# A convolution's norm steps, routed transposes and logits stand elsewhere in the order of a transformer kernel

## What is computed

```python
def conv_mixer(v, k, bias, x1, x2, num_heads):       # v = layernorm(x), x1 = x2 = ctx
    vr, x1r, x2r = (t.reshape(B, H, num_heads, L) for t in (v, x1, x2))
    kv = vr[:, :, :, None, :] * x2r[:, :, None, :, :]
    y = irfft(rfft(kv, n=2 * L) * rfft(k, n=2 * L)[None, :, None, None, :])[..., :L]
    y = y + kv * bias.reshape(H, num_heads)[None, :, :, None, None]
    return jnp.einsum('bhijl,bhil->bhjl', y, x1r).reshape(B, D, L)

x = x + conv_mixer(layernorm(x), L0_xattn_k, fside_S2_0, ctx_2048, ctx_2048, 8)
xn = layernorm(x)
logits = xn @ L0_ffn_gate_w                          # the router: the best 2 of 8 experts per row
x = x + shared_expert(xn) + routed_experts(xn, top2(logits))
x = x + latent_attention(layernorm(x), ctx_2048, itok)
x = x + ffn(layernorm(x))
```

## Time and profile before

| | before |
|---|---|
| time, median of 3 runs (lowest to highest) | 3274.34 us (3273.34 to 3274.57) |
| the profiled execution | 3277.38 us |
| its span, first to last instruction | 3275.6 us |
| PE busy | 3175.7 us (97%) |
| DVE busy | 2173.6 us (66%) |
| ACT busy | 1267.7 us (39%) |
| POOL busy | 1051.4 us (32%) |

### The profile page before, as it was taken

The page is one execution under the profiler, slowest core; times in us unless marked ns, Lnnn a source line. Parts: engine busy times, 40 slices in busy tenths (PEclk is TensorE's granted clock), DMA queues, the critical chain, the costliest instruction groups (busy, mean ns, idle before and its releaser), DMA issues.

```text
span 3275.6 us, 51687 instructions
## 1 busy us (share of the span) xinstructions
PE 3175.7 (97%) x18581; PEld 2699.7 (82%) x18581; DVE 2173.6 (66%) x5817; ACT 1267.7 (39%) x3058; POOL 1051.4 (32%) x1111
## 2 busy tenths in 40 slices
PE   7999999999999889999999999999998999999999
PEld 4666666689899769999999999999997788888887
DVE  6888888756555577778878787777776533333332
ACT  2333333333344345555555555555554311111111
POOL 7877777535211122222222222222201011010110
PEclk9999999999999899999999999999999999999999
DMA  4544443259644521111111111111101300000000
GB/s 129 155 142 133 132 140 95 81 171 313 194 155 151 207 90 53 46 46 46 46 46 40 39 46 46 46 39 40 46 14 44 108 26 26 26 26 26 26 14 13
DMA packets 123780, 267.41 MB, mean 82 GB/s; under 512 B 17689, under 2 KB 18337, under 8 KB 123530
## 3 DMA queue, kind: packets, MB, share of 16 engines
q1 hardware_dynamic: 100122, 186.59, 18.2%
q0 software_dynamic: 23408, 77.51, 7.0%
HBM read 159.49 MB, written 104.56 MB: 81 GB/s over the span
## 4 chain that ended last, share of the span: by engine, by line
PE 79%; DVE 9%; POOL 7%; ACT 1%; DMA 1%; issue 1%; SPq 0%; POOLq 0%; DVEq 0%
PE g_PH L1046 11%; PE g_O L1069 11%; PE t_U L1511 10%; PE t_S L1463 9%; PE t_PO L1498 5%; PE t_M L1447 5%; POOL c_kf L358 3%; PE t_T L1485 3%; PE f_Y L920 3%; PE f_Y L691 3%; PE t_M L1402 2%; PE f_Y L385 2%; PE f_Y L390 2%; DVE c_R L403 2%; DVE c_z L397 2%; PE t_M L1384 2%
## 5 line engine op out<-in xcount | busy, mean ns | idle before, releaser
L1473 ACT ACTIVATE t_pr<-t_sm,t_nb 128x256 f32<-128x256 f32 x512 | 256.5, 502 | 368.5 <-DVE t_nb L1469 368.5
L1059 DVE CAST g_hh<-g_hf 128x512 fp32r<-128x512 f32 x128 | 61.8, 483 | 434.7 <-PE g_O L1069 429.9
L1417 POOL TENSOR_TENSOR t_r<-t_r 128x256 f32<-128x256 f32 x128 | 95.9, 750 | 778.9 <-DVE t_rw L1479 451.7
L358 POOL TENSOR_TENSOR c_kf<-c_vt,c_ct 128x512 f32<-128x512 f32 x256 | 296.6, 1179 | 0.0
L1058 ACT ACTIVATE g_hf<-g_PH,g_b1s 128x512 f32<-128x512 f32 x128 | 88.2, 689 | 519.1 <-PE g_PH L1046 519.1
L1480 DVE TENSOR_SCALAR t_pr<-t_pr,t_rw 128x256 f32<-128x256 f32 x512 | 222.0, 434 | 18.2
L390 PE MATMUL f_Y<-c_kh,c_th 128*128 128x512 f32 x448 | 199.9, 446 | 9.6 <-ACT c_kh L365 9.6
L1046 PE MATMUL g_PH<-g_xh,g_w1h 128*128 128x512 f32 x512 | 205.3, 401 | 1.5 <-DVE g_xl L1034 1.5
L1046 PE MATMUL g_PH<-g_xh,g_w1l 128*128 128x512 f32 x512 | 203.0, 396 | 0.0
L1046 PE MATMUL g_PH<-g_xl,g_w1h 128*128 128x512 f32 x512 | 202.6, 396 | 0.0
L1069 PE MATMUL g_O<-g_w2h,g_hh 128*128 128x512 f32 x512 | 202.3, 395 | 0.0
(11 more groups left out here) (356 smaller groups left out, 9696.1 us busy)
## 6 DMA issues: line engine op xcount, KB each, us to landing
xs<-c_zero SPq DMA_DIRECT2D x71, 256.0 KB, 5.2
f_xg<-xs SPq DMA_DIRECT2D x71, 256.0 KB, 2.8
ys<-f_yt POOLq DMA_DIRECT2D x71, 256.0 KB, 2.4
c_tr<-kpad SPq DMA_DIRECT2D x60, 256.0 KB, 4.8
f_xg<-xn SPq DMA_DIRECT2D x40, 256.0 KB, 4.6
c_xt<-x SPq DMA_DIRECT2D x32, 256.0 KB, 3.5
c_cr<-ctx SPq DMA_DIRECT2D x32, 256.0 KB, 3.9
c_ct<-ctxh SPq DMA_DIRECT2D x32, 256.0 KB, 4.4
```

The source lines that it names most:

```text
L358: T["kv", h] = T["kv1", n] = p.do("gpsimd", lambda e: e.tensor_tensor(o, iv, ic, ALU.mult), g("vt", h), g("ct", h), g("kl", n - 8), g("kh" ...
L1473: T["ex", x] = p.do("scalar", lambda e, t=t, k4=k4: e.activation(pr[:, N % 2, t, :], sm[:, k4, :], ACT.Exp, bias=nb[:, k4, 0:1], scale=-1. ...
```

## The change

`layernorm_stats` is taken apart for the two norms of the convolution: the DVE part (`layernorm_variance`, its first line is 118 in the changed kernel) stays in `stats` and `stats0`, and POOL's power gets functions of its own, `power` and `power0`, that are called a step or more later. `shift(h + 1)` moves from the last step of the head before to the first of this one, `weigh` a step later, `stats` a step earlier; `shift0` and `norm0` stand together behind step 2 of the second half; `turn0` stands ahead of step 3 instead of behind it; `logit` behind step 0 of the first half instead of step 1.

```diff
+def layernorm_variance(p, x, st, ag, rs, tok, free):
+
+    a = p.do("vector", lambda e: e.bn_stats(st, x), tok, free)
+    a = p.do("vector", lambda e: e.bn_aggr(ag, st), a)
+    return p.do("vector", lambda e: e.tensor_scalar(rs, ag[:, 1:2], EPS, None, ALU.add), a)
...
+    def power0(i):
+        s = i % 2
+        U["rs", i] = p.do("gpsimd", lambda e: e.tensor_tensor(rs0[:, s, :], rs0[:, s, :], mhalf, ALU.pow), U["va", i], c_mh)
...
-                if u == 1 and lb == 2 and h + 2 < n_heads:
+                if u == 1 and lb == 1 and h + 2 < n_heads:
                     stats(h + 2)
+                if u == 1 and lb == 3 and h + 2 < n_heads:
+                    power(h + 2)
...
                 if u == 0 and lb == 0 and more:
+                    if h:
+                        shift(h + 1)
                     norm(h + 1)
-                if u == 0 and lb == 0 and more:
+                if u == 0 and lb == 1 and more:
                     weigh(h + 1)
-                if u == 1 and lb == 3 and h + 2 < n_heads:
-                    shift(h + 2)
...
+                if u == 1 and lb == 3 and h:
+                    turn0(h - 1)
                 conv(h, u, lb, units[n] if n < len(units) and lb == 0 else None)
...
+                if u == 0 and lb == 0 and h > 1:
+                    logit(h - 2)
                 if u == 0 and lb == 1:
                     shared_weights()
-                    if h > 1:
-                        logit(h - 2)
...
                 if h and u == 1:
-                    (stats0, shift0, norm0, turn0)[lb](h - 1)
+                    if lb < 3:
+                        (stats0, power0, shift0)[lb](h - 1)
+                    if lb == 2:
+                        norm0(h - 1)
```

More of the change, by code:

```diff
@@ L296, in stats, with power @@
         s = h % 2
-        T["rs", h] = layernorm_stats(p, xt[:, h % 4, :], st[:, s, :], ag[:, s, :], rs[:, s, :], mhalf, g("x", h), g("xn", h - 2), c_mh)
+        T["va", h] = layernorm_variance(p, xt[:, h % 4, :], st[:, s, :], ag[:, s, :], rs[:, s, :], g("x", h), g("xn", h - 2))
+    def power(h):
+        s = h % 2
+        T["rs", h] = p.do("gpsimd", lambda e: e.tensor_tensor(rs[:, s, :], rs[:, s, :], mhalf, ALU.pow), T["va", h], c_mh)
     def filt(h):
@@ L474, in stats0 @@
         s = i % 2
-        U["rs", i] = layernorm_stats(p, xt[:, i % 4, :], st0[:, s, :], ag0[:, s, :], rs0[:, s, :], mhalf, T["out2", i], gu("xb", i - 2), c_mh)
+        U["va", i] = layernorm_variance(p, xt[:, i % 4, :], st0[:, s, :], ag0[:, s, :], rs0[:, s, :], T["out2", i], gu("xb", i - 2))
+    def power0(i):
+        s = i % 2
+        U["rs", i] = p.do("gpsimd", lambda e: e.tensor_tensor(rs0[:, s, :], rs0[:, s, :], mhalf, ALU.pow), U["va", i], c_mh)
     def shift0(i):
@@ L705, in front_phase @@
     stats(0)
+    power(0)
     filt(0)
@@ L714, in front_phase @@
     stats(1)
+    power(1)
     shift(1)
@@ L799, in more @@
             pend.append((fetch(src), to, c, ("w1",) if to is w1f else ("w2",)))
-    events = {0: [lambda: finish(last), lambda: logit(last - 1), lambda: stats0(last), lambda: shift0(last), lambda: norm0(last)], 1: [lambda: best(last - 1)],
+    events = {0: [lambda: finish(last), lambda: logit(last - 1), lambda: stats0(last), lambda: power0(last), lambda: shift0(last), lambda: norm0(last)], 1: [lambda: best(last - 1)],
               3: [lambda: turn0(last)], 4: [lambda: logit(last)], 5: [lambda: best(last), lambda: choose(3)], 7: [ranks], 8: [offsets],
```

## The result

The changed kernel takes 3475.87 us (median of 4 runs, 3472.70 to 3476.75) against 3274.45 us; the ratio is 1.0608, 95% interval 1.0596 to 1.0621. That is 201 us more, where 160 were forecast: the sign and the place were right, the size was 41 us short and the time lies 14 us above the range.

A forecast was written before the change was run, and what follows sets the result against it. TensorE was taken as the bound, VectorE close behind. Stalls before `turn0` less 17.8 us won gave +118 us, the clock 42: 160 us on 3274.3, so 3434 us; own range 3415 to 3462, 8-in-10 range 3390 to 3462.

The forecast's parts named there:

- The place of the loss: TensorE, before `turn0` behind conv step 2 of the second half: stands still for `nm0` and `xb`, 4.30 us per ordinary head.
- the wait: TensorE's stalls before `turn0` summed over heads 1 to 31: 124.7, 6.4, 3.3 and 1.4 us.
- The powers leave GpSimd's way: GpSimd's wait for the variance, 4.07 us before one power, goes; nothing won, nothing lost.
- the clock: TensorE's clock falls to 1.2 GHz after nearly every stall: 1.4 us in each of 30 heads, 42 us, bounds 0 and 1.7.
- The case of the longer stretch: Rival: the low clock lasts for two stretches in some heads, another 30 x 1.7 us at most, up to 3485 us; chance 0.05.
- What was won: TensorE's waits before `turn` for `lg`, 14.7 us, and before `turn0`, 3.1 us, taken as won: 17.8 us.
- TensorE works nothing past the waiting transposes: Rival claimed the opposite: conv step 3 runs inside the stall and leaves 1.36 us of it, 3303 us; chance 0.02.
- VectorE was behind: Rival claimed the opposite: VectorE reaches z2 in time, leaving a 2.4 us chain, 3328 to 3370 us; chance 0.04.
- the faster case: Rival: `xb` is there when TensorE, itself late, comes to `turn0`; only gains are left, 3260 us; chance 0.03.
- The doubt about the range: Forecast's own range, 3415 to 3462 us: 0.3 us of doubt per stall is 9 us, the clock's upper bound 9 more.

The follow-up runs named there:

- filled wait: The changed kernel with 18 matmuls that nobody reads put on TensorE ahead of `turn0` in heads 1 to 30; ratio 1.0458 to the kernel before.
- untangled run: The changed kernel with `turn0` behind step 3, `shift0` and `norm0` ahead of step 2, `stats` of head h + 2 behind them; ratio 1.0070 to the kernel before.

## Why the prediction was wrong in size

- **The place of the loss** was right. `turn0` ahead of step 3 waits for VectorE to work off its queue up to `nm0` and for ScalarE's `xb`, in 31 heads, and undoing either half of the order shortens the wait by what the queue says (2.94 forecast and 3.10 measured for step 3, 1.31 and 1.31 for z2 and red2).
- **The first mis-sized term: the wait.** 135.8 us were summed, 156.9 measured. Of the 21 us, 20 are VectorE's `kl`, as the run with the power put back shows (137.3). The step that failed is "The powers leave GpSimd's way: 4.07 us of idle time there, with nothing late behind it on the path. Nothing won, nothing lost." It asked only who waits for GpSimd, and not what GpSimd would run beside once it no longer waits. The later power alone costs the kernel before 24 us. `choose` added 2.5 us to each of its waits (7.49 against 4.98) where 2.14 were forecast; with the power put back it adds 2.15 (6.48 against 4.33).
- **The second mis-sized term: the clock.** 42 us were forecast, 1.4 in a head. 201 - (157 - 18) = 62 us are left for it in the sum, TensorE's busy time grew by 61.5 us, and the filled wait gave back 49 in the time and 1.9 us in a head. The step that failed is the bound, "The loss is at most half of 3.4, 1.7 us": the slow stretch was taken as 3.4 us from its two examples, and in 17 of 31 heads it lasts 6.8. Against the 23.67 us of the filled run a head with the short stretch (25.0) loses 1.3 to 1.4 us, as forecast, and one with the long stretch (26.1) some 2.4, over the bound. The case of the longer stretch stood among the rivals, with a chance of 0.05 and as an upper end of 3485 us, but outside the range. The granted clock of the first quarter is 0.90, where 0.94 was forecast. The Trainium skill ("TensorE: Matmul & The Clock Gate", section "HAM oscillation — how this bites in real kernels") tells of a loop whose wait in every trip sent the clock down in every trip. For waits of this length that is borne out: 31 falls for 31 waits.
- **What was won** was about right: 17.8 us were forecast. The wait for `lg` is gone, and removing that wait alone, 14.7 us in the list, gives 16.
- **The rivals**: TensorE works nothing past the waiting transposes (4.98 us idle, with eight matmuls ready behind them); VectorE was behind, as taken; the faster case did not come up.
- **The doubt about the range** was too small: 0.3 us in each wait and the clock at its upper bound, 9 us each, were added as if nothing else on VectorE could change its duration. They make 3452 us; for the other 10 us up to 3462 no term is given.

## What to carry to other kernels

An instruction that waits should stand in its queue behind work that doesn't depend on the thing waited for; before moving it forward, sum what the engine it waits for has queued up to that point, not only the bare chain of dependences. An idle wait of an engine off the path can be worth keeping: ask which instructions it will run beside once the wait is gone. And count a repeated wait of TensorE with the clock: here each wait cost a further 1.9 us in a head on top of itself, and in another run waits of 1.88 us were followed by a fall in 20 of 25 ordinary heads.

## What the runs showed of the hardware

VectorE's duration depends on what GpSimd runs beside it, for instructions that read two operands from SBUF. `kl` takes 0.68 us alone, and up to 1.83 when it starts while an instruction of GpSimd runs; `w` takes 0.75 alone (one instance in the trace of before) and 1.34 in most heads of the same trace. The trace of before shows it in the first half of a head, here with GpSimd's `sk`:

```profile
316.26 1.34 DVE L328 SCALAR_TENSOR_TENSOR c_w<-c_xn,c_skip,c_cr 128x512 f32<-128x512 f32 x1
...
319.23 0.88 DVE L373 TENSOR_TENSOR c_kl<-c_kf,c_kh 128x512 fp32r<-128x512 f32 x1 [1.02 <-ACT c_kh L365]
```

```profile
315.77 1.28 POOL L349 TENSOR_TENSOR c_sk<-c_sk,c_xt 128x512 f32<-128x512 f32 x1
```

How much is lost follows from when the two start. In each of these rows VectorE's instruction ends some 0.55 us after the one of GpSimd that it found running: `w` at 317.60 and `sk` at 317.05; in the changed kernel VectorE's `kl` at 366.56 and GpSimd's at 366.02; in the untangled run 296.72 and 296.17. With starts 0.48, 0.21 and about 0 us behind GpSimd's `kl`, VectorE's takes 1.33, 1.63 and 1.83 us (the last in the early heads of the run with the later power alone). Where VectorE starts first it loses nothing: in the first half of the changed kernel's heads GpSimd's `kl` starts 0.63 us after VectorE's, and that takes 0.69. So VectorE seems to stand still until GpSimd's instruction is done. GpSimd can lose as well: its `kl` takes 1.72 us instead of 1.27 in early heads of the untangled run, where VectorE's is already under way.

`z`, which reads PSUM and SBUF, and `R`, which reads one operand, stay at 0.68 on the mean in both kernels. The Trainium skill, "SBUF — State Buffer", section "Who interferes with whom", says that a VectorE instruction with two SBUF inputs contends with a GpSimd instruction that reads SBUF, and that one with at most one SBUF input, outside the two-port modes, does not. The traces agree with that: `kl` goes from 0.68 to 1.33 us and `z` and `R` stay.

The other surprise is how little it takes to lower the clock again and again: 1.88 us of waiting in a head of 20.8 did it in 20 of 25 ordinary heads of one run and left it alone in the other five. In the untangled run even one of 18 waits of 0.70 to 0.77 us was followed by a fall (head 14, at 323.36), there behind a wait and the small matmuls of the logits. Why the slow stretch lasts 3.4 us in some heads and 6.8 in others was not settled. In the changed kernel all 17 long ones began 1.1 us or more before TensorE resumed, and the 14 short ones at most 0.63 before it or later; but with `turn0` behind step 3 and nothing to fill the wait, stretches of 6.8 us began 0.8 to 1.3 us after it.
